# Modulation vectors of an adaLN block: four of six summed over row blocks on GpSimd, then one product with ones each

## What is computed

```python
mod = (silu(c) @ wmod).reshape(1, 6, 512)          # c: 1 x 512, wmod: 512 x 3072
sa, ca, ga, sb, cb, gb = mod[:, 0], ..., mod[:, 5]
ga = (2 * (ga >= 0) - 1) * maximum(abs(ga), 0.25)  # gb likewise
h = layernorm(x) * (1 + ca) + sa
x = x + ga * attention(h, wq, wk, wv, wo)          # 32 heads, 8 key/value heads, causal, rotary
h = layernorm(x) * (1 + cb) + sb
x = x + gb * ffn(h)                                # dense + routed low-rank
```

## Time and profile before

| | us |
|---|---|
| median of 3 runs | 1106.07 (1105.58 to 1106.41) |
| profiled execution, whole | 1104.76 |
| its span in the trace | 1103.0 |
| TensorE busy | 1078.8 (98% of the span), mean granted clock 0.996 |
| VectorE busy | 747.2 (68%) |
| ScalarE busy | 641.3 (58%) |
| GpSimd busy | 514.1 (47%) |
| start of the attention's first scores | 45 |
| start of the second group's first scores | 156.6 |

### The profile page before, as it was taken

The page is one execution under the profiler, slowest core; times in us unless marked ns, Lnnn a source line. Parts: engine busy times, 40 slices in busy tenths (PEclk is TensorE's granted clock), DMA queues, the critical chain, the costliest instruction groups (busy, mean ns, idle before and its releaser), DMA issues.

```text
span 1103.0 us, 17122 instructions
## 1 busy us (share of the span) xinstructions
PE 1078.8 (98%) x5800; PEld 909.7 (82%) x5800; DVE 747.2 (68%) x1746; ACT 641.3 (58%) x1402; POOL 514.1 (47%) x505
## 2 busy tenths in 40 slices
PE   6999999999999999999999999999999999999997
PEld 2778888888888888888888888888888888888875
DVE  4768865588547865588647865688646875578676
ACT  5547764477437754478426854477535764467533
POOL 2526652365325743365424752456524662355244
PEclk8999999999999999999999999999999999999999
DMA  6440100011000110001000110001100110001001
GB/s 213 132 150 25 48 20 10 10 31 39 21 1 20 39 30 11 10 29 40 20 1 20 29 40 10 9 21 39 30 1 20 30 39 10 1 29 59 10 20 58
DMA packets 38077, 37.91 MB, mean 34 GB/s; under 512 B 3108, under 2 KB 27812, under 8 KB 37864
## 3 DMA queue, kind: packets, MB, share of 16 engines
q1 hardware_dynamic: 37992, 36.82, 10.8%
HBM read 34.72 MB, written 2.10 MB: 33 GB/s over the span
## 4 chain that ended last, share of the span: by engine, by line
PE 92%; DVE 3%; ACT 1%; DMA 1%; issue 1%; POOL 1%; SPq 0%; POOLq 0%; ACTq 0%
PE accumulators L597 22%; PE accumulators L582 19%; PE scores L545 18%; PE accumulators L612 16%; PE transposed L558 11%; PE scores L818 2%; PE accumulators L635 1%; DVE wv_lo L1201 1%; DMA qr<-in_L_attn_x_dram 1%; PE transposed L647 1%; PE scores L827 1%; PE transposed L802 1%; DVE qc L1164 1%; DMA trig<-in_L_ffn_W_dram 0%; ACT qr L882 0%
## 5 line engine op out<-in xcount | busy, mean ns | idle before, releaser
L1475 POOL TENSOR_SCALAR p_large<-p_large,rowinv 128x640 f32<-128x640 f32 (+3 forms) x128 | 125.8, 983 | 237.3 <-DVE rowinv L1132 237.3
L1139 DVE TENSOR_TENSOR pb_lo<-transposed,pb_hi 128x512 fp32r<-128x512 f32 (+3 forms) x256 | 138.9, 584 | 101.3 <-ACT pb_hi L861 101.3
L1484 POOL TENSOR_TENSOR qr<-qr,trig 128x512 f32<-128x512 f32 x80 | 104.2, 1302 | 208.3 <-ACT qr L882 208.3
L861 ACT ACTIVATE pb_hi<-transposed 128x512 fp32r<-128x512 f32 (+3 forms) x256 | 118.2, 514 | 128.8 <-PE transposed L558 127.5
L853 ACT ACTIVATE p_large<-p_large,negmax 128x640 f32<-128x640 f32 (+3 forms) x128 | 126.5, 989 | 42.2 <-DVE negmax L1127 42.1
L545 PE MATMUL scores<-k_hi,q_hi 128*128 128x512 f32 (+2 forms) x384 | 145.1, 378 | 0.0
L1127 DVE CUSTOM_DVE_ANT_0 p_large<-scores,mask 128x640 f32<-128x640 f32 (+3 forms) x128 | 128.6, 1018 | 12.5 <-PE scores L545 12.1
L1488 POOL TENSOR_TENSOR qc<-qc,qr 128x512 f32<-128x512 f32 x80 | 109.0, 1363 | 54.4 <-DVE qc L1164 50.6
L545 PE MATMUL scores<-k_hi,q_lo 128*128 128x512 f32 (+2 forms) x384 | 131.6, 343 | 0.0
L545 PE MATMUL scores<-k_lo,q_hi 128*128 128x512 f32 (+2 forms) x384 | 130.9, 341 | 0.0
L1475 POOL TENSOR_SCALAR p_small<-p_small,rowinv 128x128 f32<-128x128 f32 (+3 forms) x128 | 97.9, 782 | 31.5 <-DVE rowinv L1132 31.4
(11 more groups left out here) (167 smaller groups left out, 2366.6 us busy)
## 6 DMA issues: line engine op xcount, KB each, us to landing
stage<-in_L_attn_wq_dram SPq DMA_DIRECT2D x32, 256.0 KB, 2.7
stage<-in_L_attn_wo_dram SPq DMA_DIRECT2D x32, 256.0 KB, 2.6
y<-in_L_wmod_dram SPq DMA_DIRECT2D x4, 512.0 KB, 6.4
stage<-in_L_attn_wk_dram SPq DMA_DIRECT2D x8, 256.0 KB, 2.8
stage<-in_L_attn_wv_dram SPq DMA_DIRECT2D x8, 256.0 KB, 2.8
y<-in_L_wmod_dram SPq DMA_DIRECT2D x1, 2048.0 KB, 11.9
y<-in_L_wmod_dram SPq DMA_DIRECT2D x2, 1024.0 KB, 5.1
y<-in_L_attn_x_dram SPq DMA_DIRECT2D x1, 2048.0 KB, 8.6
```

What stands on the lines that cost most here:

```text
L861: nc.scalar.activation(pt_of(i, part, True), src, ACT.Copy).then_inc(t_hi, 1)
L1139: nc.vector.tensor_tensor(pt_of(i, part, False), src, f32(pt_of(i, part, True)), ALU.subtract).then_inc(t_lo, 1)
L1475: nc.gpsimd.tensor_scalar(row(i), row(i), rowinv[:, i:i + 1], 1.0, ALU.mult, ALU.mult).then_inc(s_norm, 1)
L1484: nc.gpsimd.tensor_tensor(qr[:, s, :], qr[:, s, :], trig[:, 1, half * HALF:(half + 1) * HALF], ALU.mult).then_inc(r_sin, 1)
```

## The change

For ga, sb, gb and cb the sum over the four row blocks moves from TensorE to GpSimd. `modulation_scale` waits for the transfer and multiplies the four blocks of 128x512 in place by their silu column; `modulation_add` adds blocks 1 to 3 to block 0, each addition waiting for the one before (`mod_step`), and signals `mod_summed`. TensorE then needs one product with ones: all 128 columns of `ones` for a gate, one column for sb and cb. The spread silu (L1241) is gone.

The jobs move too: ga stays in (0, 5), sb goes to (1, 5), gb to (2, 4), cb and "second" to (2, 5). The order of loads follows, and the load of x into `y` now waits for cb. On GpSimd the scalings stand ahead of tile 4's normalise and the additions behind it, once in each of heads 0 to 2; a second pair stands in head 1 (gb): scalings after tile 5, additions at its end.

```diff
@@ fillers
-        (0, 2): wo(0) + mod("sb"),
-        (0, 3): wo(1) + mod("cb"),
-        (0, 4): wo(2, 3) + mod("second") + [("q", (1, 0), 0)],
-        (0, 5): wo(4, 5, 6) + mod("ga", "gb") + [("q", (1, 1), 0)],
+        (0, 2): wo(0),
+        (0, 3): wo(1),
+        (0, 4): wo(2, 3) + [("q", (1, 0), 0)],
+        (0, 5): wo(4, 5, 6) + mod("ga") + [("q", (1, 1), 0)],
         (1, 1): wo(7),
         (1, 4): [("q", (2, 0), 0)],
-        (1, 5): [("q", (2, 1), 0)],
-        (2, 4): [("q", (3, 0), 0)],
-        (2, 5): [("q", (3, 1), 0)],
+        (1, 5): mod("sb") + [("q", (2, 1), 0)],
+        (2, 4): mod("gb") + [("q", (3, 0), 0)],
+        (2, 5): mod("cb", "second") + [("q", (3, 1), 0)],
@@ SP
             sp.wait_ge(a_full, N.value("a", ("mod", "ca"), g0))
-            sp.dma_start(mod_w, wmod_v[:, :, 3 * D:5 * D]).then_inc(mod_in[0], 16)
+            sp.dma_start(mod_w, wmod_v[:, :, 2 * D:4 * D]).then_inc(mod_in[0], 16)
             load(("q", 1), g0)
-            sp.wait_ge(a_full, N.value("a", ("mod", "sb"), g0))
-            sp.dma_start(mod_w[:, :, 0:D], wmod_v[:, :, 2 * D:3 * D]).then_inc(mod_in[1], 16)
-            sp.wait_ge(a_full, N.value("a", ("mod", "cb"), g0))
-            sp.dma_start(mod_w[:, :, D:2 * D], wmod_v[:, :, 5 * D:6 * D]).then_inc(mod_in[2], 16)
+            sp.wait_ge(a_full, N.value("a", ("mod", "ga"), g0))
+            sp.dma_start(mod_w[:, :, 0:D], wmod_v[:, :, 5 * D:6 * D]).then_inc(mod_in[1], 16)
             load(("q", 2), g0)
             load(("wo", 0), g0)
-            sp.wait_ge(a_full, N.value("a", ("mod", "gb"), g0))
+            load(("q", 3), g0)
+            sp.wait_ge(a_full, N.value("a", ("mod", "sb"), g0))
+            sp.dma_start(mod_w[:, :, D:2 * D], wmod_v[:, :, 4 * D:5 * D]).then_inc(mod_in[2], 16)
+            load(("wo", 1), g0)
+            load(("wo", 2), g0)
+            sp.wait_ge(a_full, N.value("a", ("mod", "cb"), g0))
             sp.dma_start(y[:], x[0].rearrange("(t p) d -> p t d", p=P)).then_inc(y_in, 16)
-            for what in W_GROUP[3:]:
-                load(what, g0)
+            load(("wo", 3), g0)
@@ TensorE, modulation
-                    for k in range(KC):
-                        mm = nc.tensor.matmul(acc if gate else acc[0:1, :],
-                                              vt[:, k * P:(k + 1) * P] if gate else silu[:, 3, k:k + 1],
-                                              mod_w[:, k, chunk * D:(chunk + 1) * D], start=(k == 0), stop=(k == KC - 1))
+                    mm = nc.tensor.matmul(acc if gate else acc[0:1, :], ones[:] if gate else ones[:, 0:1],
+                                          mod_w[:, 0, chunk * D:(chunk + 1) * D], start=True, stop=True)
@@ GpSimd
+            def modulation_scale(arrived, chunk):
+                pool.wait_ge(mod_in[arrived], 32)
+                for k in range(KC):
+                    nc.gpsimd.tensor_scalar(part(k, chunk), part(k, chunk), silu[:, 3, k:k + 1], 1.0, ALU.mult,
+                                            ALU.mult).then_inc(mod_step, 1)
+                steps[0] += KC
+            def modulation_add(chunk):
+                for k in range(1, KC):
+                    pool.wait_ge(mod_step, steps[0])
+                    ins = nc.gpsimd.tensor_tensor(part(0, chunk), part(0, chunk), part(k, chunk), ALU.add)
+                    if k < KC - 1:
+                        ins.then_inc(mod_step, 1)
+                        steps[0] += 1
+                ins.then_inc(mod_summed, 1)
@@ GpSimd, back
+                job = {0: (0, 0), 1: (0, 1), 2: (2, 1)}.get(h) if at.first else None
                 if h in (1, 2):
                     scale_wo(h - 1, at)
+                if job:
+                    modulation_scale(*job)
                 normalise(h, 4, at)
+                if job:
+                    modulation_add(job[1])
                 normalise(h, 5, at)
                 if h == 2:
                     scale_wo(2, at)
+                if at.first and h == 1:
+                    modulation_scale(1, 0)
                 rotate(("q", ((h + 1) % R, 0)), at, int(last))
                 normalise(h, 6, at)
                 normalise(h, 7, at)
+                if at.first and h == 1:
+                    modulation_add(0)
```

## The result

The changed kernel took 1113.77 us (median of 6 runs, 1113.02 to 1114.53) against 1106.24 us (1105.16 to 1107.78) for the kernel before beside it: a ratio of 1.0066, 95% interval 1.0053 to 1.0079. It is slower by 7.5 us, where 5.0 was forecast (1111.1) and 1114.5 was the rival in which the clock falls. The profiled execution took 1113.75 us, with a span of 1112.0 us against 1103.0: 9.0 us apart, more than the medians, since the profiled execution of before is a short one of its kernel.

The account below looks back on a forecast made before the run. TensorE, busy 98% of the span, was taken to bound the kernel. New waits of 3.9 + 5.4 + 6.0 = 15.3 us against 10.3 saved gave 1106.07 + 5.0 = 1111.1 us; range 1105.5 to 1115.5.

Parts of the forecast that it names:

- the rival in which the clock falls: Head 2: TensorE's wait before "second" lowers the granted clock, costing 3.4 us more, 1114.5 us; chance 0.16.
- What goes: TensorE loses three of four products of each vector, 12 x 0.86 = 10.3 us, all on the chain.
- Head 0: New TensorE waits in the first head, once covered by the removed products: sum 3.9 us.
- T0: Transposes of row tile 0 in head 0: with tile 1's, wait 1.1 us for GpSimd's normalise.
- T7: Transposes of row tile 7: wait 0.9 us in head 0 behind VectorE's gate passes, 0.4 us in head 1.
- Head 1: GpSimd, with two vectors to sum, delays TensorE: waits 4.8 us, 5.4 with meetings with VectorE.
- T5: Transposes of row tile 5 in head 1: wait 1.3 us for GpSimd's additions and normalise.
- S4 of head 2: Scores of row tile 4 in head 2: wait 2.1 us behind GpSimd's additions of gb and second rotation.
- Head 2: TensorE waits for gb's bank and for VectorE's copy of cb before "second": sum 6.0 us.
- PVa: One half of `weighted`; in head 2 it waits 2.1 us for the bank held by VectorE's gb passes.
- GpSimd keeps up: Rival: GpSimd catches up in every wait, leaving 0.4 us in head 1; no change, 1106.1 us; chance 0.12.
- faster: Rival: also, gb's bank is free when wanted in head 2; 2.7 us less, 1103.4 us; chance 0.14.

Follow-up runs that it names:

- experiment 1: Changed kernel with twelve extra dense 128x512 products on TensorE in the wait before "second": 1110.36 us, ratio 1.0043.
- experiment 9: Changed kernel with sb back on TensorE, GpSimd summing one vector a head, cb, "second" and gb moved, gb's bank freed by one copy: 1099.52 us, ratio 0.9947.
- Experiment 2: Changed kernel without GpSimd's scalings and additions, so the four vectors hold block 0 alone, unscaled: 1109.69 us, ratio 1.0037.
- 3: Changed kernel with the projection of q placed between cb and "second" in head 2: 1107.91 us, ratio 1.0022.
- 7: Changed kernel with "second" behind the projection of q and gb's bank freed early by one copy: 1109.07 us, ratio 1.0036.
- 6: Changed kernel with gb's bank freed by one copy and its four gate passes moved to the end of head 3's back half: 1113.12 us, ratio 1.0073.
- 8: Changed kernel with "second" behind the projection, gb's bank freed early and six extra dense products before "second": 1108.17 us, ratio 1.0027.
- 10: Version of experiment 9 with all three additions of a head ahead of tile 5's normalise in heads 1 and 2: 1101.41 us, ratio 0.9966.
- experiment 4: Kernel before with sb and cb each made by one product instead of four, nothing else changed: 1105.31 us, ratio 0.999.

## Why the prediction was right and wrong

The direction, the range and most places were right; the likeliest case was not the one that came.

- **What goes** (10.3 us): right. TensorE's busy time fell by only 4.0, mostly because products at the lower clock count as busy for longer (5.1 us), so "lower by about 10" was a poor sign to name.
- **Head 0**: 3.9 was forecast, and head 1 began at 67.05 where 67 was forecast. One cause was misnamed. T0 and T1 were to wait 1.1 for N0 and T2 1.8 for a bank. In the trace T0 itself waits 2.84, for the bank that `v_lo` frees. The prediction had `v_lo` in the same line of VectorE's queue but took it for T2's business only. T7 waited 0.94, as forecast (0.9).
- **Head 1**: T5 waited 0.99 (1.3 forecast) and S4 of head 2 1.61 (2.1). The waits of T4, T6 and T7, 1.4 together, did not come. Three additions took 4.0 to 4.4 us (4.1 forecast, of which the 0.07 us for each wait stood on no row). GpSimd was nearly without idle time, as foretold, but the two waits that came were 0.3 and 0.5 us shorter than chained in the prediction. Head 2 began at 93.44 where 94 was forecast.
- **Head 2**: its parts add up to 5.7 to 5.9 us, and the sum was written with 6.0. PVa waited 1.97 (2.1) and "second" 3.43 (3.6 to 3.8), with the releasers that were named. wo3's load was hidden, as argued.
- **The sum of waits** was thus 15.3 against 12.0 in rows, 13.6 with the rest: 1.7 too much.
- **The clock** is the step that failed. The forecast put it at nothing. It stood among the rivals at 0.16, with the right price for the fall behind "second" (3.4 forecast, 3.4 measured, and 3.2 to 3.4 given back in experiment 1), though the price was read from a fall at 20 us among short transposes, so its digits are partly luck. Two reasons spoke against it. "The work ahead of the wait is dense" did not protect it. That the waits in head 1 were "under 2.2 us" held for head 1 (0.99 and 1.61 us, no fall), but it said nothing of PVa's wait in head 2, behind whose 1.97 us the clock fell as well. That second fall, 1.7 us, was in no case at all. The trace of before had a fall behind 2.6 us, shorter than the wait that was forecast, so 0.16 was too low; it was no certainty either, since behind T0's 2.84 us the clock fell in three of seven traces. The Trainium skill (TensorE: Matmul & The Clock Gate, Part 1) puts the lower clock down to idle time as well, and the trace agrees for the waits (1.97 and 3.43 us); that the clock also falls where TensorE does not wait is seen in experiment 9.
- So 5.0 - 1.7 + 5.1 = 8.4 us at head 3, where 5.0 was forecast, and 1113.77 us lies above the forecast's own 1108.6 to 1113.1, in the part of the range that the fallen clock had added. Two errors of opposite sign made the number look better than its parts; in the medians 7.5 us are left of it.
- *GpSimd keeps up* and *faster* are refuted by rows. Experiment 2 adds that even free sums on GpSimd would not have made the change a gain: without them it is still 4.4 us slower than before. What is left of GpSimd's part, 3.2 to 4.1 us, is less than the clock's 5.1.

## What to carry to other kernels

Before work is taken off the engine that sets the time, ask what runs under its cover. The same 5.2 us taken out at two places was worth 2.6 us at one (in executions whose clock held) and a loss at the other, because the next consumer waits for a bank that another engine frees in a fixed order. Price each new wait of TensorE twice, once for itself and once for the clock (1.7 to 3.4 us a fall here, behind waits of 1.5 to 4.2 us), and put a step that needs another engine's copy far behind its source: one change of order gave back 5.9 us, and order, cover and one vector a head made a version 5.8 us faster than the kernel before.

## What was not expected of the hardware

- The clock can fall with no wait of TensorE near. In experiment 9 sixteen records of one-column products (1.94 us) were followed by a window at 0.66. With the same products spread between wide ones two windows read low (0.60 and 0.72).
- Whether it falls differs by kernel and execution at like places. Behind T0's 2.84 us it did not fall in the traces of after and of experiments 1, 3 and 7 and did in those of 2, 6 and 8 (about 1.4 us). Behind "second" it fell in 9 and not in 10. What decides it is open. It moves medians: the two groups of runs of experiment 4 and the 6 us spread of experiment 7 go with the mean granted clock, so a difference of under 2 us between two of these kernels can be the clock alone.
- One dense product more can be worth less than nothing in time: twelve of them, 3.06 us, made the kernel 3.4 us faster (2.5).
